# A four-layer conv/triangle kernel: one wait for PSUM banks moved, one sigmoid moved, and one layer's variance taken from whole float32 squares

## The chip, the cores and the metric

The kernel runs on one core of a Trainium2 chip. The metric is device time in microseconds (us), from the first to the last instruction and what lies around them. The median of three runs of the kernel before is 1442.51 us (1441.29 to 1446.19).

A core has five engines with instruction streams of their own, joined by semaphores: PE (TensorE, matrix products into PSUM), DVE (VectorE), ACT (ScalarE), POOL (GpSimd) and SP (the queue that starts DMAs). PSUM has eight banks.

## The reference

The image x has 192 x 192 positions of 64 channels in float32. Four layers are added to it in turn; each sees a group-normed copy. Cut to layer 1, whose kind the others share:

```
x = x + L1(_gn(x))                              # group norm, 32 groups of 2 channels
def L1(z):
    x = layernorm(z, ln_in_w, ln_in_b)          # over the 64 channels
    a = m * sigmoid(x @ w_a_g + b_a_g) * (x @ w_a_p + b_a_p)
    b = m * sigmoid(x @ w_b_g + b_b_g) * (x @ w_b_p + b_b_p)
    t = einsum('bikc,bjkc->bijc', a, b)
    t = layernorm(t, ln_out_w, ln_out_b) @ w_o + b_o
    return sigmoid(x @ w_g + b_g) * t
```

Layer 0 has the same form (its einsum in bf16), layer 2 has no mask and sums over the first index, layer 3 has no layer norm at its entry.

## The kernel before

Each layer l has three stages. **Phase A** normalises the input, makes the gate and the four projections and leaves `a` and `b` in SBUF (`lr`). **Phase b1** is the einsum, **phase b2** the second norm, the output product and the sum with x. The change touches phase A alone, and of it layers 0 to 2, which have the layer norm (`ln`).

Phase A runs over 48 tiles (`TILES`). A tile is two rows of the image (r = 0, 1), 2 x 192 positions in the free dimension; the 128 partitions are 64 channels of the upper and 64 of the lower half of the image. Each engine has a `step` that it runs for tile after tile, in an order written out by hand, which works ahead for later tiles. PE's steps are unrolled; the others loop over four tiles at a time, but for the first four and the last four. In step n:

- PE: the gate product of tile n (`gate`), the transposes that spread 1/deviation of tile n+1 over partitions (`spread`, L552), the projections of row 0 (`project(n, s, 0)`: a wide part L588, then a narrow part L598), the centring product of tile n+4 (`centre`, L520), the projections of row 1 (narrow, then wide), the variance of tile n+3 (L543).
- ACT: the gate's sigmoid (L804), `high` of tile n+1 (L821, the copy of the normalised tile that PE reads), the sigmoid of row 0 (L812), `centred` of tile n+4 (L784, writes `cen`), the sigmoid of row 1 (L812), the square of tile n+4 (L790).
- DVE: the masked product of row 1 of tile n-1 (`glu`, four instructions of L1065; L1072 in layer 2, one), variance plus epsilon of tile n+2 (L1031, `ve`), the normalising product of tile n+1 (L1041, `xn`), `sq_low` of tile n+3 (L1026), in layers 1 and 2 the low part of tile n+1 (L1048, `val`), the product of row 0 of tile n.
- POOL: the power -1/2 (L1224, `rstd`) and its spread over 64 columns (L1231, `rb`), tile n+2.

The variance on PE uses the squares (`sq`, stationary) against two columns of 1/64. So that bf16 products suffice, a square is taken as `sq_high`, the upper 16 bits of each word, and `sq_low`, the rest, which DVE computes. PE waits for it on `a_sq_lo`.

Row 0's projections lie in PSUM banks 4 and 5, row 1's in 6 and 7. `glu` of tile n frees them, and counts `a_free`: value l x 96 + m + 1 says that the row m - 2, the last user of row m's banks, is done. PE waits for it at two places: before row 0 for row 0's banks, and, in layers with a norm, before the last pass of row 0's wide part for those of row 1. Layers 1 and 2 have three passes (weights and data in high and low bf16 parts), layer 0 has one pass in float32, so that in layer 0 the first and the last pass are the same and both waits stand ahead of row 0. PE's gate product of tile n also waits for `cen` of tile n+3 (`a_cen`), since both write banks 0 and 1.

Of the kernel before, what the change touches and what calls it, by code (L numbers as in the profile page):

```python
# [25 lines left out]
P = 128  # L26
# [5 lines left out]
TILES = HALF // ROWS  # L32
# [8 lines left out]
SUBS = ROWS * TILES  # L41
GROUP = 4
GROUPS = C // GROUP
CHUNKS = TILE // P
LAYERS = 4
# [10 lines left out]
HAS_MASK = (True, True, False, True)  # L56
GATE_FIRST = (True, False, True, False)
LATE = 14
T_SCALE = (1.0, 1.0, 1.0 / N, 1.0)
Z_BANK = (0, 1, 6, 7)  # L60


def build_triangle_layers(nc, x_in, params, consts, mask3_k, mask3_row, x_out):
# [6 lines left out]
    with ExitStack() as ctx:  # L70
# [16 lines left out]
        sq = sb("sq", [P, 2, TILE])  # L87
# [52 lines left out]
        k_sel = k[:, K_SEL:K_SEL + 2]  # L140
# [331 lines left out]
        def _(pe):  # L472
# [19 lines left out]
            def phase_a(l):  # L492
# [44 lines left out]
                def variance(n, s):  # L537

                    slot_free(pe, a_ve, base + n)
                    pe.wait_ge(a_sq_lo, base + n + 1)  # L540
                    for j in range(CHUNKS):
                        for part in (sq_high, sq_low):
                            mm = nc.tensor.matmul(ps[:, 3, 2 * j:2 * j + 2],  # L543
                                                  part[:, s % 2, P * j:P * j + P], sel_bf[:, :],
                                                  start=part is sq_high, stop=part is sq_low)
                    mm.then_inc(a_var, 1)
# [27 lines left out]
                def project(n, s, r):  # L574
                    m = ROWS * n + r

                    if r == 0 or not ln:
                        pe.wait_ge(a_free, l * SUBS + m + 1)
                    banks = [ps[:, 4 + 2 * r + h, 0:2 * COLS].rearrange("p (v c) -> p v c", v=2) for h in range(2)]

                    def wide():
                        for w, x in passes:
                            start, stop = (w, x) == passes[0], (w, x) == passes[-1]
                            if ln and r == 0 and stop:

                                pe.wait_ge(a_free, l * SUBS + m + 2)
                            for h in range(2):
                                mm = nc.tensor.matmul(banks[h][:, :, 0:P], moving(x, s)[half(h), N * r:N * r + P],  # L588
                                                      proj_weights(w, h)[:, 0:2 * P], start=start, stop=stop,
                                                      skip_group_check=True)  # L590
                        return mm

                    def narrow():
                        for w, x in passes:
                            start, stop = (w, x) == passes[0], (w, x) == passes[-1]
                            for h in range(2):
                                for e in range(2):
                                    mm = nc.tensor.matmul(banks[h][TAIL * e:TAIL * e + TAIL, :, P:COLS],  # L598
                                                          moving(x, s)[half(h), N * r + P:N * r + N],
                                                          proj_weights(w, h)[:, 2 * P + P * e:3 * P + P * e],  # L600
                                                          start=start, stop=stop, skip_group_check=True)
                        return mm

                    if r == 0 or not ln:
                        wide()
                        mm = narrow()
                    else:
                        narrow()
                        mm = wide()
                    mm.then_inc(a_proj, 1)  # L610
# [161 lines left out]
        def _(act):  # L772
            def phase_a(l):
                base = l * TILES
                ln = HAS_LN[l]
                act.wait_ge(gn_dve, 7 * (l + 1))
                act.wait_ge(params_ready, l + 1)

                def centred(n, s):


                    act.wait_ge(a_z, base + n + 1)
                    slot_free(act, a_xn, base + n - RING + 1)
                    nc.scalar.activation(cen[:, s, :].rearrange("p (h j) -> p h j", h=2), ps[:, 0:2, 0:N], ACT.Identity,  # L784
                                         bias=gn_cb).then_inc(a_cen, 1)

                def squared(n, s):
                    act.wait_ge(a_cen, base + n + 1)
                    slot_free(act, a_var, base + n - 1)
                    nc.scalar.activation(sq[:, s % 2, :], cen[:, s, :], ACT.Square).then_inc(a_sq, 1)  # L790

                def plain(n, i, s):

                    act.wait_ge(in_loaded[s], in_count(l, s) + 16 * (i + 1))
                    slot_free(act, a_proj, l * SUBS + ROWS * (n - 1))
                    nc.scalar.activation(xn[:, s % 2, :], in_ring[:, s, :], ACT.Identity, bias=gn_b, scale=gn_a)\
                        .then_inc(a_xn, 1)

                def gate(n, i, s):
                    act.wait_ge(a_gate_mm, base + n + 1)  # L800

                    slot_free(act, gate_stored[s], 16 * (l * TURNS + i))
                    slot = gate_ring[:, s, :].rearrange("p (r j) -> p r j", r=ROWS)
                    nc.scalar.activation(slot if ln else gate_ring[:, s, :], ps[:, 0:2, N:2 * N] if ln else ps[:, 3, 0:TILE],  # L804
                                         ACT.Sigmoid, bias=gate_bias[:, 0:1]).then_inc(a_gate, 1)

                def sigmoids(n, s, r):
                    m = ROWS * n + r
                    act.wait_ge(a_proj, l * SUBS + m + 1)

                    act.wait_ge(a_free, l * SUBS + m + 1)
                    nc.scalar.activation(act_out[:, r, :].rearrange("p (h c) -> p h c", h=2),  # L812
                                         ps[:, 4 + 2 * r:6 + 2 * r, COLS:2 * COLS], ACT.Sigmoid).then_inc(a_sig, 1)

                def high(n, s):


                    act.wait_ge(a_xn, base + n + 1)
                    slot_free(act, a_proj, l * SUBS + ROWS * (n - 1))
                    out = xn_parts[:, s % 2, 0, :] if IN_PARTS[l] else val[:, s % 2, :]  # L820
                    nc.scalar.activation(out, xn[:, s % 2, :], ACT.Copy, bias=1.0).then_inc(a_hi, 1)  # L821

                def step(n, i, s, ahead):
                    gate(n, i, s)
                    if ln and ahead >= 1:
                        high(n + 1, (s + 1) % RING)
                    sigmoids(n, s, 0)
                    if ln and ahead >= 4:
                        centred(n + 4, s)
                    sigmoids(n, s, 1)  # L830
                    if ln and ahead >= 4:
                        squared(n + 4, s)
                    if not ln and ahead >= 2:
                        plain(n + 2, i + (s + 2) // RING, (s + 2) % RING)

                if ln:
                    for n in range(RING):
                        centred(n, n)
                        squared(n, n)
                    high(0, 0)  # L840
                else:
                    plain(0, 0, 0)
                    plain(1, 0, 1)
                over_tiles(act, step)
# [90 lines left out]
        def _(dve):  # L935
# [79 lines left out]
            def phase_a(l):  # L1015
                base = l * TILES
                ln = HAS_LN[l]
                out5 = lr_view(l).rearrange("p a e (h r) -> p h a e r", h=2)
                mask4 = mask[:, :, :].rearrange("p t (h r) -> p t h r", h=2)
                if l:  # L1020
# [56 lines left out]
                def step(n, i, s, ahead):  # L1077
                    if not (isinstance(n, int) and n == 0):
                        glu(n - 1, 1)
                    if ln and ahead >= 2:  # L1080
                        var_eps(n + 2, (s + 2) % RING)
                    if ln and ahead >= 1:
                        normalise(n + 1, (s + 1) % RING)
                    if ln and ahead >= 3:
                        square_low(n + 3, (s + 3) % RING)
                    if IN_PARTS[l] and ahead >= 1:
                        low(n + 1, (s + 1) % RING)
                    glu(n, 0)

                if ln:  # L1090
                    square_low(0, 0)
                    square_low(1, 1)
                    var_eps(0, 0)
                    var_eps(1, 1)
                    normalise(0, 0)
                    square_low(2, 2)
                if IN_PARTS[l]:
                    low(0, 0)
# [283 lines left out]
```

## Time and profile before

| | |
|---|---|
| median of the runs | 1442.51 us |
| time of the profiled execution, its span | 1443.26 us, 1441.0 us |
| PE, PEld, DVE, ACT, POOL busy | 82%, 47%, 68%, 63%, 36% |
| phase A of layer 0, of layer 1, of layer 2 | some 50 to 252 us, 393 to 581 us, 780 to 961 us |
| granted TensorE clock, mean | 0.962 |

"PEld" is the loading of weights into PE, which overlaps its products. A group's idle time is that of its engine just before it, with what ended it. Times of single instructions come from the timeline, whose stamps count from the start of the span. In the timeline instructions of one line that follow each other are merged into one row (x4, x8).

### The profile page before, as it was taken

To read this page: it belongs to the slowest core of one execution; us is meant where nothing else is said; L and a number is where in the kernel's file an instruction comes from. 1 tells how busy PE (TensorE), PEld (TensorE's weight loads), DVE (VectorE), ACT (ScalarE), POOL (GpSimd) and SP (SyncE) were. 2 spreads that over 40 slices of the span, in tenths; PEclk is the share of its full clock that TensorE was granted. 3 is DMA by queue.
4 is the path that set the end of the run, shared out by engine and by line. 5 is a ranking of instruction groups with operands and counts; after the bars stand their busy time and mean duration, and the time that the engine had idled before them with its cause. 6 is when DMAs were issued, how large, how long until landed. Compare 5 with 4: busy or idle time off the path is not lost. (4 is left out here: it accounts for less than half of the span.)

```text
span 1441.0 us, 43510 instructions
## 1 busy us (share of the span) xinstructions
PE 1182.2 (82%) x13502; PEld 679.1 (47%) x13502; DVE 978.2 (68%) x2692; ACT 905.7 (63%) x1849; POOL 524.0 (36%) x490
## 2 busy tenths in 40 slices
PE   0688887889778887999982888889888788899887
PEld 0355554444344444674431555557544344467443
DVE  6577777368789999226991877752299799931577
ACT  0566676389677776126992877752399677732676
POOL 0355554035465565003551666630055300000355
PEclk9999999899889999999995989999999899999999
DMA  8011111678633332697658555549889544459898
GB/s 293 23 51 51 45 51 51 153 213 265 208 97 110 111 103 82 200 298 216 200 162 323 159 160 155 168 138 297 274 279 286 189 154 153 153 175 314 272 303 272
DMA packets 222489, 259.67 MB, mean 180 GB/s; under 512 B 54176, under 2 KB 209056, under 8 KB 222368
## 3 DMA queue, kind: packets, MB, share of 16 engines
q1 hardware_dynamic: 193920, 232.75, 51.5%
q10 hardware_dynamic: 28448, 25.17, 5.3%
q8 instruction: 92, 1.51, 0.4%
q14 instruction: 29, 0.24, 0.1%
HBM read 139.89 MB, written 117.96 MB: 179 GB/s over the span
## 5 line engine op out<-in xcount | busy, mean ns | idle before, releaser
L1065 DVE SCALAR_TENSOR_TENSOR lr<-ps,mask,act_out 128x128 f32 (+5 forms) x1152 | 281.8, 310 | 66.8 <-ACT act_out L812 59.5
L1224 POOL TENSOR_TENSOR rstd<-ve,half_col 128x6 f32<-128x6 f32 x144 | 190.4, 1322 | 248.8 <-DVE ve L1031 247.4
L588 PE MATMUL ps<-w_parts,val 64*128 64x256 bf16 (+1 forms) x1728 | 202.5, 312 | 47.5 <-DVE lr L1065 47.4
L1269 POOL TENSOR_TENSOR new_ring<-val,lr 128x384 f32<-128x384 f32 x96 | 103.8, 1083 | 375.9 <-issue 301.4
L812 ACT ACTIVATE act_out<-ps 128x384 f32<-128x384 f32 x384 | 186.2, 487 | 52.0 <-PE ps L598 35.4
L1257 POOL TENSOR_TENSOR val<-act_out,gate_ring 128x384 f32<-128x384 f32 x96 | 100.1, 1043 | 221.7 <-ACT act_out L883 190.2
L821 ACT ACTIVATE val<-xn 128x384 bf16<-128x384 f32 (+1 forms) x144 | 75.3, 523 | 123.4 <-PE ps L598 63.0
L703 PE MATMUL ps<-in_ring,k 128*128 128x384 f32 x288 | 123.6, 514 | 26.2 <-DMA in_ring<-t_scratch 21.8
L866 ACT ACTIVATE sq<-ps 128x384 f32<-128x384 f32 x192 | 104.6, 545 | 53.1 <-PE ps L703 51.2
L1116 DVE COPY cen<-ps 128x384 f32<-128x384 f32 x48 | 26.7, 557 | 161.8 <-PE ps L661 161.8
L661 PE MATMUL ps<-lr 64*128 64x192 f32 (+3 forms) x896 | 128.3, 334 | 10.0 <-DVE lr L1065 5.2
L588 PEld LDWEIGHTS ps<-w_parts,val 64*128 64x128 bf16 (+1 forms) x1728 | 81.1, 115 | 111.1 <-DVE lr L1065 70.7
L1231 POOL TENSOR_TENSOR rb<-rstd,one_col 128x384 f32<-128x384 f32 x144 | 127.2, 884 | 11.3
L598 PE MATMUL ps<-w_parts,val 64*64 64x128 bf16 (+1 forms) x3456 | 130.4, 238 | 0.0
L1129 DVE TENSOR_TENSOR xn<-ps,rb 128x384 f32<-128x384 f32 x192 | 106.0, 552 | 32.3 <-ACT rb L877 31.8
L872 ACT ACTIVATE rb<-ps,eps_col 128x384 f32<-128x384 f32 x192 | 120.0, 625 | 9.5 <-PE ps L715 5.8
L661 PEld LDWEIGHTS ps<-lr 64*128 64x128 f32 (+3 forms) x896 | 105.9, 181 | 29.8 <-issue 18.4
L784 ACT ACTIVATE cen<-ps,gn 128x384 f32<-128x384 f32 x144 | 82.9, 576 | 52.4 <-PE ps L520 52.2
L804 ACT ACTIVATE gate_ring<-ps,gate_bias 128x384 f32<-128x384 f32 x192 | 111.2, 579 | 3.2 <-PE ps L520 2.7
L877 ACT ACTIVATE rb<-rb 128x384 f32<-128x384 f32 x192 | 109.4, 570 | 0.3
L598 PEld LDWEIGHTS ps<-w_parts,val 64*64 64x64 bf16 (+1 forms) x3456 | 84.2, 115 | 39.3 <-issue 25.0
L1158 DVE TENSOR_TENSOR sq_low<-sq 128x384 bf16<-128x384 f32 x144 | 79.7, 553 | 33.2 <-ACT sq L866 33.0
(110 smaller groups left out, 2195.0 us busy)
## 6 DMA issues: line engine op xcount, KB each, us to landing
gate_scratch<-gate_ring SPq DMA_DIRECT2D x192, 192.0 KB, 2.3
gate_ring<-gate_scratch SPq DMA_DIRECT2D x96, 384.0 KB, 3.9
lr<-x_scratch SPq DMA_DIRECT2D x72, 384.0 KB, 4.9
in_ring<-t_scratch SPq DMA_DIRECT2D x72, 384.0 KB, 3.8
x_scratch<-new_ring SPq DMA_DIRECT2D x48, 384.0 KB, 3.2
in_ring<-x_scratch SPq DMA_DIRECT2D x96, 192.0 KB, 2.4
lr<-x SPq DMA_DIRECT2D x6, 1536.0 KB, 15.5
t_scratch<-cen SPq DMA_DIRECT2D x96, 96.0 KB, 4.1
```

The costliest lines, as they stand in the source:

```text
L588: mm = nc.tensor.matmul(banks[h][:, :, 0:P], moving(x, s)[half(h), N * r:N * r + P], proj_weights(w, h)[:, 0:2 * P], start=start, stop=sto ...
L598: mm = nc.tensor.matmul(banks[h][TAIL * e:TAIL * e + TAIL, :, P:COLS], moving(x, s)[half(h), N * r + P:N * r + N], proj_weights(w, h)[:, 2 ...
L661: mm = nc.tensor.matmul(ps[:, b + i % 2, N * (i // 2):N * (i // 2) + N], left[:, 0:P], right, start=first and i < 2, stop=last and i >= 2, ...
L703: nc.tensor.matmul(ps[:, Z_BANK[s], 0:TILE], w_c, t_slots(l, s)[:, 0, :], start=True, stop=True).then_inc(b2_z, 1)
L804: nc.scalar.activation(slot if ln else gate_ring[:, s, :], ps[:, 0:2, N:2 * N] if ln else ps[:, 3, 0:TILE], ACT.Sigmoid, bias=gate_bias[:, ...
L812: nc.scalar.activation(act_out[:, r, :].rearrange("p (h c) -> p h c", h=2), ps[:, 4 + 2 * r:6 + 2 * r, COLS:2 * COLS], ACT.Sigmoid).then_i ...
L872: nc.scalar.activation(rb[:, s % 2, :], ps[:, 2 + s % 2, 0:TILE], ACT.Ln, bias=eps_col[:, l:l + 1]).then_inc(b2_log, 1)
L877: nc.scalar.activation(rb[:, s % 2, :], rb[:, s % 2, :], ACT.Exp, scale=-0.5).then_inc(b2_rstd, 1)
L1065: ins = nc.vector.scalar_tensor_tensor(out5[:, h, lo // 2:hi // 2, :, row], ps[:, 4 + 2 * r + g, lo:hi].rearrange("p (a e) -> p a e", e=2) ...
L1129: nc.vector.tensor_tensor(xn[:, s % 2, :], ps[:, Z_BANK[s], 0:TILE], rb[:, s % 2, :], ALU.mult)\
L1224: nc.gpsimd.tensor_tensor(rstd[:, s % 2, :], ve[:, s % 2, :], half_col[:, :], ALU.pow)\
L1231: nc.gpsimd.tensor_tensor(rb[:, s % 2, :].rearrange("p (a c) -> p a c", c=C), rstd[:, s % 2, :].rearrange("p (a o) -> p a o", o=1) .broadc ...
```

## The change

1. In `project`, the wait for row 1's banks moves from ahead of the last pass of row 0's wide part to ahead of row 1's projections.
2. In ACT's step, in layer 0 alone, the sigmoid of row 0 comes before `high` of the next tile.
3. In layer 1, PE takes the variance from the whole float32 squares: three float32 products per tile instead of six in bf16, waiting for ACT's square (`a_sq`). DVE makes no `sq_low` there.

```diff
+WHOLE_VAR = (False, True, False, False)
+LOWS = tuple(sum(1 for m in range(l) if not WHOLE_VAR[m]) for l in range(LAYERS))
...
                     slot_free(pe, a_ve, base + n)
-                    pe.wait_ge(a_sq_lo, base + n + 1)
+                    if WHOLE_VAR[l]:
+                        pe.wait_ge(a_sq, base + n + 1)
+                        for j in range(CHUNKS):
+                            mm = nc.tensor.matmul(ps[:, 3, 2 * j:2 * j + 2], sq[:, s % 2, P * j:P * j + P], k_sel,
+                                                  start=True, stop=True)
+                        mm.then_inc(a_var, 1)
+                        return
+                    pe.wait_ge(a_sq_lo, LOWS[l] * TILES + n + 1)
...
                     m = ROWS * n + r
-                    if r == 0 or not ln:
-                        pe.wait_ge(a_free, l * SUBS + m + 1)
+                    pe.wait_ge(a_free, l * SUBS + m + 1)
...
                             start, stop = (w, x) == passes[0], (w, x) == passes[-1]
-                            if ln and r == 0 and stop:
-
-                                pe.wait_ge(a_free, l * SUBS + m + 2)
...
                     gate(n, i, s)
+                    if l == 0:
+                        sigmoids(n, s, 0)
                     if ln and ahead >= 1:
                         high(n + 1, (s + 1) % RING)
-                    sigmoids(n, s, 0)
+                    if l:
+                        sigmoids(n, s, 0)
...
+                halved = ln and not WHOLE_VAR[l]
...
-                    if ln and ahead >= 3:
+                    if halved and ahead >= 3:
                         square_low(n + 3, (s + 3) % RING)
...
-                if ln:
+                if halved:
                     square_low(0, 0)
                     square_low(1, 1)
+                if ln:
                     var_eps(0, 0)
                     var_eps(1, 1)
                     normalise(0, 0)
+                if halved:
                     square_low(2, 2)
```

The next two lists are PE's stream in one step of layer 0, before and changed: the gate product of a tile (`val,w_gate`), the spread (`k,rb`), row 0, the centring (`lr,w_centre`), row 1. Line numbers of the changed kernel are higher by up to nine.

```order
L520 MATMUL ps<-val,w_gate 64x192 [waits a_cen,a_hi]
L520 MATMUL ps<-val,w_gate 64x192 x3
L552 MATMUL ps<-k,rb 128x128 [waits a_xn,a_rb]
L552 MATMUL ps<-k,rb 128x128 x2
L588 MATMUL ps<-w_parts,val 128x2x128 [waits a_free]
L588 MATMUL ps<-w_parts,val 128x2x128
L598 MATMUL ps<-w_parts,val 64x2x64 x4
L520 MATMUL ps<-lr,w_centre 64x192 [waits a_gate,a_cen]
L520 MATMUL ps<-lr,w_centre 64x192 x3
L598 MATMUL ps<-w_parts,val 64x2x64 x4
L588 MATMUL ps<-w_parts,val 128x2x128 x2
```

```order
L522 MATMUL ps<-val,w_gate 64x192 [waits a_cen,a_hi]
L522 MATMUL ps<-val,w_gate 64x192 x3
L561 MATMUL ps<-k,rb 128x128 [waits a_xn,a_rb]
L561 MATMUL ps<-k,rb 128x128 x2
L593 MATMUL ps<-w_parts,val 128x2x128 [waits a_free]
L593 MATMUL ps<-w_parts,val 128x2x128
L603 MATMUL ps<-w_parts,val 64x2x64 x4
L522 MATMUL ps<-lr,w_centre 64x192 [waits a_gate,a_cen]
L522 MATMUL ps<-lr,w_centre 64x192 x3
L603 MATMUL ps<-w_parts,val 64x2x64 [waits a_free]
L603 MATMUL ps<-w_parts,val 64x2x64 x3
L593 MATMUL ps<-w_parts,val 128x2x128 x2
```

The order of the products stays. The first `a_free` wait is still there but asks for one row less, and a second one stands behind the centring, ahead of row 1.

ACT's stream in one step of layer 0's loop, before and changed:

```order
L804 ACTIVATE gate_ring<-ps,gate_bias 128x384 [waits gate_stored1,a_gate_mm]
L266 REGISTER_ALU [waits a_xn]
L821 ACTIVATE val<-xn 128x384 [waits a_proj]
L809 REGISTER_ALU
L812 ACTIVATE act_out<-ps 128x384 [waits a_free,a_proj]
L782 REGISTER_ALU
L784 ACTIVATE cen<-ps,gn 128x384 [waits a_xn,a_z]
```

```order
L809 ACTIVATE gate_ring<-ps,gate_bias 128x384 [waits gate_stored1,a_gate_mm]
L814 ISA
L817 ACTIVATE act_out<-ps 128x384 [waits a_free,a_proj]
L826 ACTIVATE val<-xn 128x384 [waits a_proj,a_xn]
L787 REGISTER_ALU
L789 ACTIVATE cen<-ps,gn 128x384 [waits a_xn,a_z]
```

The sigmoid of row 0 (`act_out`) now stands ahead of `high` (`val<-xn`), and `cen` directly behind `high`.

PE's stream at the end of a step of layer 1, from the last projections over the variance to the next gate, before and changed:

```order
L588 MATMUL ps<-w_parts,val 128x2x128 x6
L543 MATMUL ps<-sel_bf,sq 128x2 [waits a_sq_lo,a_ve]
L543 MATMUL ps<-sel_bf,sq_low 128x2
L543 MATMUL ps<-sel_bf,sq 128x2
L543 MATMUL ps<-sel_bf,sq_low 128x2
L543 MATMUL ps<-sel_bf,sq 128x2
L543 MATMUL ps<-sel_bf,sq_low 128x2
L520 MATMUL ps<-val,w_gate_parts 64x192 [waits a_cen,a_lo]
```

```order
L593 MATMUL ps<-w_parts,val 128x2x128 x6
L545 MATMUL ps<-k,sq 128x2 [waits a_sq,a_ve]
L545 MATMUL ps<-k,sq 128x2 x2
L522 MATMUL ps<-val,w_gate_parts 64x192 [waits a_cen,a_lo]
```

Nothing moves here: the variance stays where it was, with three float32 products in the place of six.

## Rows read from the trace of the kernel before

**Rows 1.** Page, costliest groups: busy us, mean ns | idle before, releaser.
```profile
L588 PE MATMUL ps<-w_parts,val 64*128 64x256 bf16 (+1 forms) x1728 | 202.5, 312 | 47.5 <-DVE lr L1065 47.4
```

**Rows 2.** Windows, layer 0: us; busy PE, PEld, DVE, ACT, POOL; clock; DMA share; GB/s.
```profile
60.00:230.00 170.00, 142.35 (x2013) 86.26 (x2013) 124.17 (x455) 117.49 (x248) 88.71 (x83) 1.00 0.14 49
```

**Rows 3.** Timeline, layer 0, product of row 0: tiles 0, 43 and 47.
```profile
57.56 0.99 DVE L1065 SCALAR_TENSOR_TENSOR lr<-ps,mask,act_out 128x128 bf16<-128x128 f32 x4 [1.14 <-ACT act_out L812]
...
235.33 2.01 DVE L1065 SCALAR_TENSOR_TENSOR lr<-ps,mask,act_out 128x128 f32 x8 [0.96 <-ACT act_out L812]
...
250.29 1.89 DVE L1065 SCALAR_TENSOR_TENSOR lr<-ps,mask,act_out 128x128 bf16<-128x128 f32 x8 [1.82 <-ACT act_out L812]
```

**Rows 4.** Timeline, one step of layer 0: start us, us, instruction [idle before <-releaser].
```profile
145.11 0.21 PEld L520 LDWEIGHTS ps<-val,w_gate 64*64 64x64 f32 x8
...
145.59 0.31 PEld L552 LDWEIGHTS ps<-k,rb 128*128 128x128 f32 x3 [0.28 <-issue]
...
145.66 0.99 DVE L1065 SCALAR_TENSOR_TENSOR lr<-ps,mask,act_out 128x128 f32 x4 [0.17 <-ACT act_out L812]
...
146.57 0.15 DVE L1031 TENSOR_SCALAR ve<-ps 128x6 f32<-128x6 f32 x1
...
146.77 0.33 PEld L588 LDWEIGHTS ps<-w_parts,val 64*128 64x128 f32 x4 [0.86 <-DVE lr L1065]
...
147.30 0.52 ACT L821 ACTIVATE val<-xn 128x384 f32<-128x384 f32 x1 [0.94 <-DVE xn L1041]
147.43 0.21 PEld L598 LDWEIGHTS ps<-w_parts,val 64*64 64x64 f32 x8 [0.33 <-issue]
...
147.95 0.49 ACT L812 ACTIVATE act_out<-ps 128x384 f32<-128x384 f32 x1
...
148.21 0.83 POOL L1231 TENSOR_TENSOR rb<-rstd,one_col 128x384 f32<-128x384 f32 x1
148.34 0.57 ACT L784 ACTIVATE cen<-ps,gn 128x384 f32<-128x384 f32 x1
...
149.10 0.49 ACT L812 ACTIVATE act_out<-ps 128x384 f32<-128x384 f32 x1 [0.19 <-PE ps L588]
...
149.22 0.21 PEld L520 LDWEIGHTS ps<-val,w_gate 64*64 64x64 f32 x8
```

**Rows 5.** Timeline, one step of layer 1.
```profile
502.68 0.26 PEld L520 LDWEIGHTS ps<-val,w_gate_parts 64*64 64x64 bf16 x12 [0.45 <-DVE val L1048]
...
503.08 0.31 PEld L552 LDWEIGHTS ps<-k,rb 128*128 128x128 f32 x3
...
503.56 0.11 PEld L588 LDWEIGHTS ps<-w_parts,val 64*128 64x128 bf16 x4 [0.17 <-issue]
...
504.21 0.10 PEld L588 LDWEIGHTS ps<-w_parts,val 64*128 64x128 bf16 x2 [0.54 <-DVE lr L1065]
...
504.61 0.55 DVE L1026 TENSOR_TENSOR sq_low<-sq 128x384 bf16<-128x384 f32 x1
...
504.82 0.52 ACT L821 ACTIVATE val<-xn 128x384 bf16<-128x384 f32 x1 [0.99 <-PE ps L598]
...
505.25 0.47 ACT L812 ACTIVATE act_out<-ps 128x384 f32<-128x384 f32 x1
...
505.37 0.56 DVE L1048 SCALAR_TENSOR_TENSOR val<-xn,val 128x384 bf16<-128x384 f32 x1 [0.22 <-ACT val L821]
505.62 0.57 ACT L784 ACTIVATE cen<-ps,gn 128x384 f32<-128x384 f32 x1
505.65 0.10 PEld L543 LDWEIGHTS ps<-sel_bf,sq 128*128 128x128 bf16 x1 [0.21 <-issue]
...
506.31 0.26 PEld L520 LDWEIGHTS ps<-val,w_gate_parts 64*64 64x64 bf16 x12 [0.44 <-DVE val L1048]
```

**Rows 6.** Source line L480 (ns min/median/max); timeline of its two weight loads.
```profile
L480 PEld LDWEIGHTS ps<-cols,w_out x8: 191/192/333, 10.1 to 993.0; 128*128 128x128 f32 x8
...
615.77 0.30 PEld L480 LDWEIGHTS ps<-cols,w_out 128*128 128x128 f32 x2
```

## Prediction

> **What bounds the kernel now.** I read the costliest groups of the page first, to see where TensorE stands idle, and then the timeline of one step in layer 0 and in layer 1. The projections of line L588 are preceded by 47.5 us of idle PE time, 47.4 of it waits for the masked product L1065, which only layers 0 and 1 have [rows 1]; layer 2 (L1072) has the other 0.1, so nothing is to be had there. In layer 0 PE runs at a granted clock of 1.00 and is busy 142 of 170 us [rows 2], yet every tile costs the same 4.1 us, so some chain is closed.
>
> The timeline of layer 0 names it [rows 4]. I call G the gate matmuls (PEld L520 at 145.11), S the spread (L552, 145.59), W0 and N0 the wide and narrow parts of row 0 (L588 at 146.77, L598 at 147.43), N1 and W1 those of row 1, sig0 and sig1 the two L812, glu0 and glu1 the two L1065. W0 stands idle 0.86 us and starts 0.12 after glu1 of the previous tile ends (145.66 + 0.99 = 146.65). From W0 the chain runs through all of the projection to sig1 (149.10, 2.33 after W0), and the next glu1 stands one period after 145.66, at 149.77: 0.12 + 2.33 + 0.67 + 0.99 = 4.11 us. That is the period G to G (145.11 to 149.22). A single wait, put on row 0 for banks that only row 1 uses, closes it. ACT's high (L821) adds nothing on that chain, but it stands ahead of sig0 and waits for DVE's xn.
>
> In layer 1 the chain is another one [rows 5]. DVE's low (L1048, 505.37) waits for ACT's high (504.82), and sq_low (504.61, 0.55 long, over at 505.16) lies wholly in that time: DVE is idle 0.22 us between the two. sig0 (505.25) follows high by 0.43. The period, 506.31 − 502.68 = 3.63 us, is closed by DVE and this one trip to ACT: xn, high, low, glu0, glu1, and back. PE waits twice in it, at the third pass of row 0 (504.21, 0.54 us of idle weight load) and at the gate (506.31, 0.44), which stands 0.12 after cen (505.62 + 0.57), so I take cen for its releaser and not low.
>
> **Layer 0, the moved wait and the moved sigmoid.** W0 now waits for glu0 of the previous tile only. That ended before glu1 began (145.66), so W0 follows S. Layer 0 has no row for W0 unhindered; layer 1 has S to W0 = 503.56 − 503.08 = 0.48. PE's own work per tile is then 4.11 less the wait: 146.77 − (145.59 + 0.48) = 0.70, so 3.41 us. What is late next? The gate of the next tile waits for cen (L784), and cen now stands behind sig0 and high:
> - G to S 0.48, S to W0 0.48, W0 to N0 0.66, N0 to sig0 0.52 (147.95 − 147.43) [rows 4];
> - sig0 to high: back-to-back activations start 0.39 apart (147.95 to 148.34); high to the next one 0.43 (504.82 to 505.25) [rows 4, 5];
> - cen itself 0.57, and its release of the gate 0.12: 506.31 − (505.62 + 0.57) [rows 5].
>
> Sum 0.48 + 0.48 + 0.66 + 0.52 + 0.39 + 0.43 + 0.57 + 0.12 = 3.65 us. Other loops are shorter. Row 1's new wait stands behind N0 (G + 1.62) and the centre's matmuls; glu1 stands at (sig0 + 0.39 + 0.43 + 0.46) + 0.67 = G + 4.09 and ends at G + 5.08, which is 1.43 after the next G: before N0 even begins (0.46 for cen to sig1 is my estimate, between 0.43 and cen's own 0.57). Behind that wait stand N1, W1, the variance and the next gate, and nobody pays. The long path over POOL: ve to the end of rb is 149.04 − 146.57 = 2.47; ve starts 0.91 after glu1, at G + 5.00, so rb is there at G + 7.56, and the spread that wants it stands at 2 × 3.65 + 0.48 = 7.78. It fits by 0.2 us, and would bind at about 3.55. DVE's work is 124.2 us in 170, or 3.0 per tile [rows 2]. high is ready 0.73 after ve starts (147.30 − 146.57), at G + 5.73 − 3.65 = 2.08, and now starts at G + 2.53, so xn is waited for no more. High before sig0 would have put sig0 behind DVE's xn, so the moved sigmoid is part of the gain.
>
> How many tiles: glu0 of tile 0 stands at 57.56, of tile 43 at 235.33, of tile 47 at 250.29 [rows 3]. 43 steps average 4.134; 43 × (4.134 − 3.65) = 20.8 us. The last four steps have no centre; they took 14.96 us. There POOL's path comes in sight, I put them at 13.5, 1.4 less. Layer 0: **−22.2 us**.
>
> **Layer 1, sq_low and the whole squares.** DVE loses 48 sq_low of 0.55 us, 26 us of work, and I give it **nothing**: it is covered by ACT's high, and without it the wait before low grows from 0.22 to about 0.7 us. PE trades six bf16 products of two columns for three float32 ones. Nearest row: the product L480, 128×128 against one column, two loads in 0.30 us where a single one takes 0.19, so a load every 0.11 us; at the lower clock, where a load takes 0.33, I take twice that, 0.22 [rows 6]. Six loads are 0.66, with 0.09 for the turn to the gate 0.75 us. The room: the third pass no longer waits, so the variance moves from 505.65 to about 505.25 (0.40 is my estimate, less than the 0.54 of that row). cen lets the gate go at 506.31: room 1.06, need 0.75. **0 us**, with 0.3 to spare. Without the moved wait the room would be 0.66 and the gate 0.1 late. Bounds: below nothing is excluded, since no DVE or ACT instruction of the chain gets shorter; above, see the rivals. Every 0.1 us past 1.06 costs 4.4 us over the 44 steps that have a gate waiting for cen.
>
> Before the loop of layer 1 two variances at the slow clock stand on PE ahead of the first spread: 2 × 6 × 0.22 = 2.6 us against 0.3, partly in waits for POOL and with two sq_low gone; I put +0.7. At its end row 0 of the last tile no longer waits for glu1: −0.7. Together 0 ± 1.5.
>
> A rule that speaks against the change: the Trainium skill, "FP8 and Floating Point Precision", TensorE Precision Notes, says that a true float32 product takes four passes through the array. By that rule a product would have four loads, not two, and the sum would be the second rival's. The row of L480 lists two loads for it, not four.
>
> **The sum.** The profiled execution took 1443.26 us (span 1441.0), the median of the runs is 1442.51. 1443.3 − 22.2 + 0 = 1421.1, and on the scale of the median 1420.3. I say 1420.5.
>
> **Rivals.**
> - Less in layer 0, 1429: each of three ACT instructions that now waits in a row pays some 0.07 more in the loop, where register work stands between them, and the period is 3.85. For: DVE's L1065 starts 0.67 − 0.49 = 0.18 after the sigmoid ends. Against: 0.39 holds in the same loop. 43 × 0.28 + 1.4 = 13.6. Chance 0.14.
> - Dearer float32 products, 1436: 12 loads × 0.11 + 0.09 = 1.41 us, 0.35 past the room, 44 × 0.35 = 15 back. Chance 0.04.
> - **Slower**, 1478: the same place, but each of 12 loads keeps PE for its whole 0.19: 2.37 us, 1.31 past the room, 57 us back against 22. It decides from 1.06 + 22.2/44 = 1.56 us per variance. Against it: L480's loads start 0.11 apart. Chance 0.03.
> - PE alone bounds layer 0, 1410: 43 × (4.134 − 3.41) + 1.4 = 32.5. Needs cen earlier by 0.24. Chance 0.05.
> - The wait gives nothing, since row 1 waits at once for the same glu1: 1442. That would need glu1 to end some 0.5 us later than I placed it. Chance 0.02.
>
> My forecast (period 3.55 to 3.75, 1416 to 1426) has 0.72. The range 1413 to 1432 takes in the first rival and half of the fast one. A measurement tells 0.3% (4.3 us) from no change; faster is the forecast and the rivals at 1429, 1436 and 1410, 0.95, less 0.02 for a mechanism that I did not see: 0.93; same 0.03, slower 0.04.
>
> **What would show it.** In the after profile: layer 0's G to G 3.65; W0 with no wait for L1065; PE idle about 0.24 before the gate, released by ACT cen; sig0 ahead of high. Layer 1: period 3.63 as before, DVE idle 0.7 before low, the variance in six loads over about 0.66. It would be wrong if the first projection still waits for L1065, if layer 0's period is over 3.8, or if in layer 1 PE has no wait left and the period is over 3.7.

## The result and the profile after

The changed kernel took 1422.47 us (median of 4 runs, 1419.38 to 1431.3), the kernel before 1441.9 us in the same job (4 runs, 1438.09 to 1446.19). The ratio is 0.9862, with a 95% interval of 0.9826 to 0.9898: 1.4% faster. The forecast was 1420.5 us in a range of 1413 to 1432. The profiled execution took 1419.38 us, of which the span is 1417.1, so it is 23.9 us shorter than the one before; the mean granted clock was 0.962 in both. One execution of e5 below, its profiled one (1456.07 us), was in a slower state than all others; e5's ratio leaves it out, and of its profile only rows at the full granted clock are read.

From the page of the kernel after come the span, the engines' busy time and the two groups that answer to [rows 1] (busy us, mean ns | idle before, releaser):

```profile
span 1417.1 us, 43403 instructions
PE 1197.3 (84%) x13502; PEld 704.8 (50%) x13502; DVE 954.9 (67%) x2644; ACT 898.2 (63%) x1849; POOL 522.8 (37%) x490
L1074 DVE SCALAR_TENSOR_TENSOR lr<-ps,mask,act_out 128x128 f32 (+5 forms) x1152 | 282.0, 311 | 42.5 <-ACT act_out L817 34.8
L593 PE MATMUL ps<-w_parts,val 64*128 64x256 bf16 (+1 forms) x1728 | 194.0, 313 | 0.6 <-DVE lr L1074 0.5
```

The projections now stand behind 0.6 us of idle PE time, where they stood behind 47.5. DVE has 48 instructions fewer (2644 against 2692), the halving subtractions of layer 1.

The windows view of layer 0 after, with the columns of [rows 2]:

```profile
60.00:220.00 160.00, 152.48 (x2168) 92.33 (x2164) 132.77 (x487) 118.83 (x262) 94.98 (x89) 1.00 0.16 56
```

PE is busy 95% of the time where it was 84% (142.35 of 170), at the same granted clock of 1.00. The timeline of the products of row 0, tiles 0, 43 and 47, answers to [rows 3]:

```profile
57.61 0.99 DVE L1074 SCALAR_TENSOR_TENSOR lr<-ps,mask,act_out 128x128 bf16<-128x128 f32 x4 [1.13 <-ACT act_out L817]
...
213.92 2.12 DVE L1074 SCALAR_TENSOR_TENSOR lr<-ps,mask,act_out 128x128 f32 x8 [0.37 <-ACT act_out L817]
...
226.60 1.89 DVE L1074 SCALAR_TENSOR_TENSOR lr<-ps,mask,act_out 128x128 bf16<-128x128 f32 x8 [0.83 <-ACT act_out L817]
```

43 steps average (213.92 − 57.61)/43 = 3.635 us, and the last four take 12.68. From tile 0 to tile 47 that is 168.99 us against 192.73, 23.7 us less. That the span is 23.9 us shorter, nearly the same, is partly luck: between phase A of layer 0 and that of layer 1 the execution after took 2.0 us longer than the one before, and between those of layers 1 and 2 it took 3.4 us less, in stages that the change doesn't touch. One step of layer 0, the timeline that answers to [rows 4]:

```profile
145.27 0.82 POOL L1242 TENSOR_TENSOR rb<-rstd,one_col 128x384 f32<-128x384 f32 x1
...
145.76 0.24 PEld L522 LDWEIGHTS ps<-val,w_gate 64*64 64x64 f32 x8 [0.23 <-issue]
145.79 0.56 PE L522 MATMUL ps<-val,w_gate 64*64 64x192 f32 x8 [0.17 <-ACT cen L789]
146.21 0.99 DVE L1074 SCALAR_TENSOR_TENSOR lr<-ps,mask,act_out 128x128 f32 x4 [0.28 <-ACT act_out L817]
146.28 0.31 PEld L561 LDWEIGHTS ps<-k,rb 128*128 128x128 f32 x3 [0.28 <-POOL rb L1242]
146.76 0.30 PEld L593 LDWEIGHTS ps<-w_parts,val 64*128 64x128 f32 x4 [0.17 <-issue]
...
147.39 0.21 PEld L603 LDWEIGHTS ps<-w_parts,val 64*64 64x64 f32 x8 [0.33 <-issue]
...
147.91 0.49 ACT L817 ACTIVATE act_out<-ps 128x384 f32<-128x384 f32 x1 [0.92 <-PE ps L603]
148.29 0.52 ACT L826 ACTIVATE val<-xn 128x384 f32<-128x384 f32 x1
...
148.71 0.57 ACT L789 ACTIVATE cen<-ps,gn 128x384 f32<-128x384 f32 x1
148.83 0.83 POOL L1242 TENSOR_TENSOR rb<-rstd,one_col 128x384 f32<-128x384 f32 x1
149.17 0.49 ACT L817 ACTIVATE act_out<-ps 128x384 f32<-128x384 f32 x1
149.39 0.24 PEld L522 LDWEIGHTS ps<-val,w_gate 64*64 64x64 f32 x8 [0.23 <-issue]
```

Read it down the chain. W0 (146.76) starts 0.48 after the spread and waits for nobody, though glu1 of the tile before (146.21) is only half done. sig0 (147.91) stands ahead of high (148.29), and cen (148.71, over at 149.28) is followed 0.11 later by the next gate, which the PE row names as released by cen. The period is 149.39 − 145.76 = 3.63 us.

One step of layer 1, the timeline that answers to [rows 5], and the source view of the float32 variance (ns min/median/max) in place of [rows 6]:

```profile
474.83 0.26 PEld L522 LDWEIGHTS ps<-val,w_gate_parts 64*64 64x64 bf16 x12 [0.63 <-DVE val L1057]
...
475.71 0.22 PEld L593 LDWEIGHTS ps<-w_parts,val 64*128 64x128 bf16 x6 [0.17 <-issue]
...
476.98 0.52 ACT L826 ACTIVATE val<-xn 128x384 bf16<-128x384 f32 x1 [1.00 <-DVE xn L1050]
477.36 0.74 PEld L545 LDWEIGHTS ps<-k,sq 128*128 128x128 f32 x6 [0.21 <-issue]
...
477.53 0.56 DVE L1057 SCALAR_TENSOR_TENSOR val<-xn,val 128x384 bf16<-128x384 f32 x1 [0.69 <-ACT val L826]
477.78 0.57 ACT L789 ACTIVATE cen<-ps,gn 128x384 f32<-128x384 f32 x1
...
478.46 0.26 PEld L522 LDWEIGHTS ps<-val,w_gate_parts 64*64 64x64 bf16 x12 [0.36 <-DVE val L1057]
478.49 0.44 PE L522 MATMUL ps<-val,w_gate_parts 64*64 64x192 bf16 x12 [0.30 <-ACT cen L789]
```
```profile
L545 PEld LDWEIGHTS ps<-k,sq x288: 186/192/338, 373.6 to 547.9; 128*128 128x128 f32 x144
```

All three passes of W0 go at once, one group of six loads. DVE is idle 0.69 us before low where it was idle 0.22: the time of sq_low has become a wait for ACT. The variance takes 0.74 us and the gate still waits 0.36 after it. The row of its weight load names low, over at 478.09; cen is over at 478.35, 0.11 before the gate, and the row of its products names cen. The period is unchanged, 478.46 − 474.83 = 3.63 us. Every fourth step is longer (gate sigmoid to gate sigmoid 3.63, 3.63, 3.68, 3.91, before and after alike): that is the edge of the loop, whose body holds four tiles.

### The profile page after: what moved, and what is told of

It is laid out like the page before. It is cut to its first block and busy times, and to the rows that moved or that the text cites. A ratio compares the mean times of both kernels' runs of the same rounds, so it can differ in the third digit from the quotient of the medians.

```text
span 1417.1 us, 43403 instructions
## 1 busy us (share of the span) xinstructions
PE 1197.3 (84%) x13502; PEld 704.8 (50%) x13502; DVE 954.9 (67%) x2644; ACT 898.2 (63%) x1849; POOL 522.8 (37%) x490
## 5 line engine op out<-in xcount | busy, mean ns | idle before, releaser
L593 PE MATMUL ps<-w_parts,val 64*128 64x256 bf16 (+1 forms) x1728 | 194.0, 313 | 0.6 <-DVE lr L1074 0.5
L593 PEld LDWEIGHTS ps<-w_parts,val 64*128 64x128 bf16 (+1 forms) x1728 | 79.9, 115 | 47.5 <-issue 33.3
```

## The experiments

A step below is always from one gate sigmoid to the next at the full granted clock. Medians of different jobs are compared by their ratios to the kernel before in the same job, never directly.

**The change taken apart: e1 to e4.** e1 is the kernel before with the moved wait alone.

```diff
-                    if r == 0 or not ln:
-                        pe.wait_ge(a_free, l * SUBS + m + 1)
+                    pe.wait_ge(a_free, l * SUBS + m + 1)
...
-                            if ln and r == 0 and stop:
-                                pe.wait_ge(a_free, l * SUBS + m + 2)
```

> The moved wait alone, with the kernel before's order on ACT and its variance. Theory (two loops compete in layer 0): W0 stands behind S, but high stays ahead of sig0 and waits for DVE's xn, so the period becomes xn to high 0.66, high to sig0 0.43, sig0 to glu0 0.66, glu0 to glu1 0.95, glu1 to xn 0.98 = 3.68 us, and DVE's loop edge shows again (0.3 per four tiles): about 3.75, 43 x 0.38 = 16 us and the tail. I expect -15 to -19 us, some 1424. Rival (the wait alone is the whole gain, ACT's order is nothing): period 3.63, -20 to -22 us, and ACT cen releases the gate. Second rival (the wait and the sigmoid are both needed): period over 4.0, less than -5 us.

Measured: 1425.06 us against 1444.12, ratio 0.9873 (0.9857 to 0.9888). Its timeline, the gate of one step in layer 0:

```profile
143.43 0.57 ACT L780 ACTIVATE cen<-ps,gn 128x384 f32<-128x384 f32 x1
...
144.12 0.24 PEld L520 LDWEIGHTS ps<-val,w_gate 64*64 64x64 f32 x8 [0.22 <-issue]
144.15 0.56 PE L520 MATMUL ps<-val,w_gate 64*64 64x192 f32 x8 [0.16 <-ACT cen L780]
...
146.70 0.52 ACT L817 ACTIVATE val<-xn 128x384 f32<-128x384 f32 x1 [1.28 <-DVE xn L1037]
```

The wait alone already reaches the period of 3.62, closed by cen. From the first gate sigmoid of layer 0 to the last it took 174.63 us, the kernel before 192.97 and the changed one 170.46. The 4.2 us between e1 and the changed kernel lie in one step of four, the loop's edge: it takes 3.98 to 4.04 us in e1, 3.55 in the changed kernel. The last row shows what it is: at the edge high waits 1.28 us for DVE's xn, and sig0 and cen stand behind high; in the other steps high waits 0.90 us and PE's row 0 releases it. So the expectation had the size (some 1424) and a part of the mechanism: xn is the wait in one step of four, cen in the other three.

e2 is the kernel before with the moved sigmoid alone.

```diff
+                    if l == 0:
+                        sigmoids(n, s, 0)
                     if ln and ahead >= 1:
                         high(n + 1, (s + 1) % RING)
-                    sigmoids(n, s, 0)
+                    if l:
+                        sigmoids(n, s, 0)
```

> Only the order on ACT in layer 0: sig0 ahead of high, the wait where it was. Theory: the loop of 4.11 us (glu1, W0, all of the projection, sig1, glu1) stays, and sig1 is now behind sig0, high and cen: W0 + 0.66 + 0.52 + 0.39 + 0.43 + 0.46 = W0 + 2.46 instead of 2.33, so the period is 4.24 and the kernel 0.13 x 43 = 5 us slower, 1447. Rival (sig0 earlier always helps): period under 4.11, faster.

Measured: 1449.1 us, ratio 1.0035 (1.0019 to 1.0051). By itself this part of the change costs 5 us, as expected. The waits view of its layer 0 (60 to 220 us; us in total, times, longest) and two rows of its timeline:

```profile
PEld ps L588 <- DVE lr L1068: 28.0, 38, 0.8
```
```profile
143.80 0.24 PEld L520 LDWEIGHTS ps<-val,w_gate 64*64 64x64 f32 x8 [0.23 <-issue]
...
148.02 0.24 PEld L520 LDWEIGHTS ps<-val,w_gate 64*64 64x64 f32 x8 [0.23 <-issue]
```

The period is 4.22: the loop over glu1 is still closed. Its sig1 follows W0 by 2.44 us (145.35 to 147.79) where it was 2.33, for in the new order high and cen start after sig0 and sig1 after them.

e3 is the whole float32 squares alone, e4 the wait and the sigmoid without them (all four entries of `WHOLE_VAR` False).

> Only layer 1's variance from whole float32 squares, without sq_low; wait and order as before. Theory (sq_low is covered by ACT's high; the float32 loads lie in PE's wait for cen): layer 1's period stays 3.63, DVE's idle before low grows from 0.22 to 0.7, the gate comes up to 0.15 late and nobody pays: 1442 +- 2. Rival (DVE's work counts): 44 x 0.48 = -21 us. Second rival (the float32 loads eat more than the room of 0.66): period up by 0.1 or more, +4 us or more.

> The change without its part in layer 1: moved wait and moved sigmoid, six bf16 products and sq_low in layer 1. Theory: all of the gain is layer 0's, so it is like the changed kernel: layer 0's period 3.63, layer 1's 3.63, -20 to -22 us, 1420 to 1423. Rival (the whole squares carry part of the gain): less than -17 us, with layer 1 longer than in the changed kernel by 4 us or more.

Measured: e3 1446.74 us, ratio 1.0017 (1.0003 to 1.0032); e4 1424.42 us, ratio 0.9853 (0.9834 to 0.9873). Between e4 and the changed kernel (0.9862, 0.9826 to 0.9898) the intervals show no difference: the whole gain is layer 0's. The squares give nothing, and by themselves they cost a little: e3's interval lies above 1, by 0.4 to 4.6 us.

The profiles show where. In e3 the steps of layer 1's loop are as before (four take 14.84 us, before 14.85), so what the float32 variance took beyond its six bf16 products cost no time there. The cost lies ahead of the loop and in its first steps. From the layer's first `cen` to its first gate sigmoid it takes 10.7 us in each of the seven profiles with whole squares here and below (e5 not counted), and 9.8 us in each of the six without. The first four steps took 14.54, 16.98 and 17.30 us in three profiles with whole squares (the changed kernel, after_again below, e3), and 14.40 to 15.05 in the four without them and with the same orders in layer 1 (before, e1, e2, e4). In these steps the granted clock differed, which the windows views of the same part of the loop show, first the kernel before, then e3:

```profile
404.00:418.00 14.00, 12.54 (x262) 7.69 (x260) 13.01 (x44) 10.51 (x25) 7.47 (x8) 0.93 0.33 100
```
```profile
406.00:420.00 14.00, 14.00 (x201) 9.47 (x198) 8.69 (x30) 9.06 (x20) 6.01 (x6) 0.67 0.23 69
```

The changed kernel had 4.42 and 3.26 us in the first two steps in one execution, and 5.75 and 4.59 in another (run again as after_again); over the 10 us from the first gate on the mean granted clock was 0.89 in the one and 0.58 in the other. So the clock rises at different moments with the same program. That part of the cost can't be given a size from a single profile; the 0.9 us ahead of the first gate can.

**How much room the float32 variance has: e5.** The three products are issued twice.

```diff
-                        for j in range(CHUNKS):
+                        for j in list(range(CHUNKS)) * 2:
```

> The changed kernel with the three float32 variance products of layer 1 made twice (the second set writes the same numbers). Theory (PE has a room of 1.06 us in layer 1's period, and beyond it every 0.1 us costs 4.4): the step's work up to the variance is 2.53 in the changed kernel's trace, 12 loads at 0.11 and the turn make 1.4 to 1.5, so the period is 3.95 to 4.05, 0.3 to 0.4 over 3.63: +10 to +16 us on the changed kernel, 1431 to 1438. Rival (PE has ample room): no change. Rival (each load keeps PE for 0.19): period over 4.7, +45 us.

Measured: 1433.5 us against 1439.61, ratio 0.9961 (0.9943 to 0.9979), which is 0.0099, or some 14 us, above the changed kernel's 0.9862, as expected (10 to 16). Two rows at the full granted clock:

```profile
522.41 1.42 PEld L545 LDWEIGHTS ps<-k,sq 128*128 128x128 f32 x12 [0.21 <-issue]
523.84 0.23 PEld L522 LDWEIGHTS ps<-val,w_gate_parts 64*64 64x64 bf16 x12
```

The gate follows at once and waits for nobody: twelve loads are past the room, by 0.3 us (3.93 against 3.63 in a plain step). Four steps take 15.73 us, four times 3.93, against 14.85: where PE closes the loop, its edge costs nothing, and the mean step is 0.22 us longer. In the changed kernel cen lets the gate go 478.46 − 477.36 = 1.10 us after the variance starts, and its six loads need 0.74.

**Is DVE's idle time before low worth anything: e6 to e8.** In e6 layer 1 too has the sigmoid ahead of high, and DVE does low behind the product of row 0 instead of ahead of it.

```diff
-                    if l == 0:
+                    if l <= 1:
                         sigmoids(n, s, 0)
...
-                    if l:
+                    if l > 1:
                         sigmoids(n, s, 0)
...
+                    if l == 1 and ahead >= 1:
+                        glu(n, 0)
+                        low(n + 1, (s + 1) % RING)
+                        return
```

> The changed kernel, and in layer 1 also sig0 ahead of high on ACT, and on DVE low of the next tile behind glu0 instead of ahead of it. Theory (DVE's trip to ACT and back closes layer 1's loop): glu0 now covers ACT's high, DVE's idle 0.69 before low goes, the period falls from 3.63 to what PE needs, 2.53 + 0.75 + 0.1 = about 3.35 (DVE's own work is 3.0): 44 x 0.28 = 12 us and part of the loop edges, 1406 to 1411. Rival (another wait takes its place: the gate then waits for low, which stands 1 us later): period 3.6, no change. Rival: slower than the changed kernel, since low ends only at glu0 + 0.95 + 0.56 and PE's gate waits on it.

Measured: 1430.14 us, ratio 0.9937 (0.9913 to 0.9961). I had expected 12 us less and got a layer 1 that is 11 us longer (184.19 from first to last gate sigmoid, the changed kernel 173.02). The last rival held, that low ends too late and the gate waits for it. Its timeline:

```profile
474.12 0.99 DVE L1074 SCALAR_TENSOR_TENSOR lr<-ps,mask,act_out 128x128 f32 x4 [0.76 <-ACT act_out L817]
...
475.03 0.55 DVE L1057 SCALAR_TENSOR_TENSOR val<-xn,val 128x384 bf16<-128x384 f32 x1
...
475.63 0.23 PEld L522 LDWEIGHTS ps<-val,w_gate_parts 64*64 64x64 bf16 x12 [0.62 <-DVE val L1057]
```

The gate now waits for low. The loop is glu0 to low 0.91, low to gate 0.60, gate to spread 0.37, to W0 0.48, to N0 0.43, to sig0 0.42, to glu0 0.66: 3.87 us. The wait before low is gone, and a longer loop has been bought for it: 3.87 us in a plain step where it was 3.63, and 15.48 in four steps where it was 14.85. e7 is e6 with `WHOLE_VAR` False again, e8 is e6 with the same orders in layer 2.

> The previous kernel with the bf16 variance and sq_low back in layer 1. Theory (the whole squares give nothing while high covers sq_low, but they do where it is laid open): DVE's work per tile is 3.0 + 0.48 = 3.5 and the loop edge shows, so the period is 3.5 to 3.55 against 3.35: 6 to 9 us slower than the previous kernel. Rival (sq_low stays hidden): equal within 2 us. Second rival (PE bounds, and six bf16 products are 0.5 shorter): faster than the previous kernel.

> As the kernel with low late in layer 1, and the same two orders in layer 2, whose variance stays in bf16. Theory: layer 2 waits in part for its gathered input (DMA), its steps that don't are 3.24 us with PE waiting 0.4 for cen; 0 to -6 us on the kernel with low late in layer 1. Rival: layer 2 is bounded by its DMA throughout, no change within 1 us.

Measured: e7 1423.04 us (0.9893, 0.9856 to 0.993) with the same period of 3.87, e8 1430.42 us (0.9943, 0.9915 to 0.997). e8's layer 2 took 166.35 us from first to last gate sigmoid, e6's 164.33 and e7's 166.21, so the orders gave nothing there. e7 was expected slower than e6 and its layer 1 is not (182.19): with the loop over PE closed at 3.87, sq_low is hidden once more. Its median is 7 us below e6's, though their intervals meet. Some 2.8 us of that are the price of the whole squares at the layer's start: e7 has 0.9 us less ahead of the first gate and 1.9 less in the first four steps (16.16 against 18.01). The rest stays open.

**Filling the time of high: e10 to e12.** If DVE's loop xn, high, low, glu0, glu1 closes layer 1, half of glu1 can be done while ACT makes high. e10 cuts the product of row 1 in two, one half ahead of ve and xn, one behind, and has PE do the variance ahead of row 1's projection. after_again is the changed kernel in the same job.

```diff
+                    if l == 1 and ahead >= 3:
+                        variance(n + 3, (s + 3) % RING)
                     project(n, s, 1)
-                    if ln and ahead >= 3:
+                    if ln and l != 1 and ahead >= 3:
                         variance(n + 3, (s + 3) % RING)
...
-                        glu(n - 1, 1)
+                        glu(n - 1, 1, (0,) if l == 1 else (0, 1))
...
                         normalise(n + 1, (s + 1) % RING)
+                    if tail and l == 1:
+                        glu(n - 1, 1, (1,))
```

> The changed kernel once more, as the measure for the two beside it: 1419 to 1425, 20 to 22 us below the kernel before; periods of 3.63 in layers 0 and 1.

> The changed kernel with two orders changed in layer 1: on DVE the masked product of row 1 is split, two instructions ahead of ve and xn and two behind xn, where they cover ACT's high; on PE the variance stands ahead of row 1's projections. Theory: the loop xn, high, low, glu0, glu1 loses the 0.48 us of the two moved instructions; what is then late is PE's own work, 2.53 + 0.83 = 3.36, and the loop from W1 over sig1, half of glu1 and xn back to the wait of N1 is 3.24. Period 3.36 to 3.45, 44 x 0.2 = 8 to 12 us faster than the changed kernel, about 1412. Rival (N1 now waits for the late half of glu1, as the gate did for low in the other order): period 3.63 or more, no gain or up to 6 us slower.

> The previous kernel with six bf16 products and sq_low in layer 1. Theory (once high's time is filled, sq_low is no longer covered, and the whole squares pay): DVE's work is 3.0 + 0.48 = 3.5 us a tile and its loop edge adds 0.3 every four, so the period is 3.5 to 3.6: 4 to 9 us slower than the previous kernel. Rival (PE's load was the bound, bf16 is 0.5 shorter): faster than the previous kernel.

Measured: after_again 1419.1 us (0.9844, 0.9793 to 0.9895), e10 1412.11 us (0.9821, 0.9773 to 0.987), e11, which is e10 with the halved squares, 1424.37 us (0.9897, 0.9866 to 0.9929). One step of e10 in layer 1, DVE's rows, then ACT's and the weight loads:

```profile
475.98 0.54 DVE L1077 SCALAR_TENSOR_TENSOR lr<-ps,mask,act_out 128x128 f32 x2 [0.21 <-ACT act_out L819]
...
476.51 0.56 DVE L1052 TENSOR_TENSOR xn<-ps,cen 128x384 f32<-128x384 f32 x1
476.99 0.54 DVE L1077 SCALAR_TENSOR_TENSOR lr<-ps,mask,act_out 128x128 f32 x2
477.76 0.56 DVE L1059 SCALAR_TENSOR_TENSOR val<-xn,val 128x384 bf16<-128x384 f32 x1 [0.23 <-ACT val L828]
```
```profile
471.60 0.23 PEld L522 LDWEIGHTS ps<-val,w_gate_parts 64*64 64x64 bf16 x12 [0.21 <-issue]
...
471.71 0.49 ACT L819 ACTIVATE act_out<-ps 128x384 f32<-128x384 f32 x1 [0.34 <-PE ps L593]
...
472.10 0.52 ACT L797 ACTIVATE sq<-cen 128x384 f32<-128x384 f32 x1
...
472.51 0.57 ACT L811 ACTIVATE gate_ring<-ps,gate_bias 128x384 f32<-128x384 f32 x1
472.88 0.20 PEld L603 LDWEIGHTS ps<-w_parts,val 64*64 64x64 bf16 x12 [0.21 <-issue]
...
473.19 0.24 PEld L522 LDWEIGHTS ps<-in_ring,w_centre 64*64 64x64 f32 x8
...
473.71 0.74 PEld L545 LDWEIGHTS ps<-k,sq 128*128 128x128 f32 x6 [0.28 <-issue]
...
474.47 0.20 PEld L603 LDWEIGHTS ps<-w_parts,val 64*64 64x64 bf16 x12
...
474.76 0.22 PEld L593 LDWEIGHTS ps<-w_parts,val 64*128 64x128 bf16 x6
...
475.19 0.24 PEld L522 LDWEIGHTS ps<-val,w_gate_parts 64*64 64x64 bf16 x12 [0.21 <-issue]
...
475.31 0.49 ACT L819 ACTIVATE act_out<-ps 128x384 f32<-128x384 f32 x1 [0.24 <-PE ps L593]
```

DVE's idle time before low is 0.23 us, not 0.69. The gate waits for nobody, the steps are 3.60 us each and the long fourth one is gone, so four steps take 14.40 us instead of 14.85. The forecast was a period of 3.36 to 3.45, bounded by PE. It is not PE alone that bounds it now, but a loop of PE and ACT. The centring product waits for the gate's sigmoid (`a_gate`), since both products write banks 0 and 1; ACT makes that sigmoid behind sig1 and the square. The rows give the loop: sig1 to square 0.39, to gate sigmoid 0.41, its 0.57 and 0.11 to the centring product, to variance 0.52, to N1 0.76, to W1 0.29, to the next sig1 0.55: 3.60 us. In the steps of e10 from 440 to 480 us the centring product stands 0.11 or 0.12 after the end of that sigmoid each time, and 0.29 to 0.32 after N0. In the changed kernel it stands 0.26 to 0.31 after the sigmoid and 0.14 after N0, so that it waits for nobody there. With 0.17 us less for this wait PE's own work in e10 is 3.42 us, near the expected 3.36; the new place of the variance costs it some 0.06. What the sigmoid ahead of the square would give was not run.

Whether e10 as a whole beats the changed kernel the medians don't settle, for the intervals overlap; what is shown is 0.11 us per step of layer 1, some 5 us over 44 steps, of which the slow first steps (6.07, 5.90, 4.36) take back most in this execution (172.67 us for the layer, the changed kernel 173.02). The mean granted clock in the 10 us from its first gate on was 0.50.

Between e10 and e11 the whole squares have a worth at last: the steps of e11 are 3.86, 3.87, 3.86 and 3.98, layer 1 took 180.68 us, 8.0 more. The expected period was 3.5 to 3.6, from DVE's own work, and that was not the reason. With the variance ahead of row 1, PE waits there for sq_low, and row 1 waits behind it:

```profile
475.75 0.16 PE L552 MATMUL ps<-sel_bf,sq 128*128 128x2 bf16 x1 [0.86 <-DVE sq_low L1037]
```

The loop is sig1 to glu1 0.67, to xn 0.53, to the second half of glu1 0.47, to sq_low 0.45, to variance 0.67, to N1 0.24, to W1 0.30, to sig1 0.54: 3.87 us. So the worth of the whole squares here is that sq_low drops out of this loop, which the variance's place had closed.

e12 has PE's part of e10 alone.

> The changed kernel with only PE's part of the split: in layer 1 the variance stands ahead of row 1's projections; DVE's order as in the changed kernel. Theory (the split product opened DVE's loop, and the variance's new place costs PE about 0.3 us a tile, since the narrow products of row 0, the centring and those of row 1 no longer overlap): PE's work is 3.60, still under DVE's loop, so layer 1's steps are 3.63, 3.63, 3.68, 3.91 as in the changed kernel, within 2 us of it. Rival (the variance's place alone gave the 3.60 without a loop edge): layer 1 shorter by 4 us. Rival (PE and DVE now stop each other): steps of 3.7 or more.

Measured: 1420.82 us against 1439.56, ratio 0.9872 (0.9839 to 0.9905). Four steps take 14.92 us (3.63, 3.71, 3.81, 3.77), the changed kernel's 14.85: the sum is the expected one, the single steps are not. The order on PE by itself gives nothing, so the split product is needed for e10's 3.60. Whether it would do as well with the variance in its old place was not run. In e12 the gate's sigmoid is over 0.17 to 0.30 us before the centring product, and N0 to centring is 0.14 in most steps, although the variance stands in e10's place. So that place is not what made the 0.31 of e10.

## Why the prediction was right, point by point

- **Layer 0's period.** Forecast 3.65, measured 3.635 over 43 steps. The terms: G to S 0.52 (0.48), S to W0 0.48 (0.48), W0 to N0 0.63 (0.66), N0 to sig0 0.52 (0.52), sig0 to high 0.38 (0.39), high to cen 0.42 (0.43), cen 0.57 (0.57), release 0.11 (0.12). The next wait was the one named, cen's.
- **POOL's path.** "It fits by 0.2 us" held, and was tight: rb is over at 146.09 (145.27 + 0.82), the spread starts at 146.28, and the profile names rb as its releaser. It costs nothing yet: G to S is 0.52 only because the gate's loads start 0.03 ahead of its products here, and from the products it is 0.49 (145.79 to 146.28), as before (145.11 to 145.60). The forecast's own terms for rb add up to G + 7.47 (5.00 + 2.47), not 7.56; the rows show 7.59.
- **The tail.** Forecast 13.5 for the last four steps, measured 12.68. Without the centre's matmuls the products stand 3.49, 3.20, 3.27 and 2.72 us apart. With the loop that made layer 0 23.7 us shorter against 22.2.
- **The moved sigmoid.** "High before sig0 would have put sig0 behind DVE's xn, so the moved sigmoid is part of the gain": this step was right for one step in four and wrong for the rest. e1 has the old order and the same 3.62 in a plain step, since xn was early enough; at the loop's edge its high does wait for xn. What the move gives is that edge, some 4 us in the profiled layer 0, and by itself it costs 5 (e2). In the runs e1 and e4 can't be told apart (0.9873 and 0.9853).
- **sq_low, nothing.** Held: DVE idle 0.69 before low (0.7), the period 3.63, and e4 without this part is as fast.
- **The float32 variance.** Six loads in 0.74 (0.66 forecast, and 0.09 for the turn), room 1.10 (1.06), start at G + 2.53 (2.57). The rivals with twelve loads fell by the row of L545, two loads a product; e5 shows that with twelve loads the period would have been 3.93, by the sum of the prediction 3.63 + 1.41 − 1.06 = 3.98. The rule of the Trainium skill, "FP8 and Floating Point Precision", TensorE Precision Notes, on four passes for a true float32 product does not show here as four weight loads: the view lists 288 of them for 144 products.
- **Layer 1's ends.** Put at +0.7 and −0.7, together 0 ± 1.5. Both held: the start, first `cen` to first gate sigmoid, grew from 9.82 to 10.71 us, and the end, last gate sigmoid to the end of the last product, fell from 4.36 to 3.67. Missing was a term for the steps behind the first gate: the first four took 0.1 us more in the profiled execution and 2.6 more in after_again.
- **The sum.** Forecast −22.2 in a profiled execution; the spans differ by 23.9, the medians by 19.4. Layer 0 alone gave 23.7 against 22.2, of which 0.7 is the period and 0.8 the tail. The interval of the ratio, times 1441.9, is 14.7 to 25.1 us and holds both.

## What to carry to other kernels

A wait written for two users of a buffer belongs in front of the one whose data it guards: one wait for banks of the second row, put before the first, closed a loop over three engines and cost 18 us of 1441, though no engine was full. Work taken from an engine that waits at once for another (sq_low) buys nothing while no closed loop runs through it; before moving an instruction to fill it, add up the loop that its consumer closes, as e6's 3.87 shows. A row marked with no wait can still hide one, when the engine's next rows overlap: e10's centring product was found only by setting its start beside the end of what it waits for. Where parts of a change touch the same loop, time each alone: here one gave some 18 us, one cost 5 us alone and gave up to 4 behind the other, and the third gave nothing and cost a little at the layer's start.

## What the runs showed that was not expected

- A float32 load of 128×128 takes 0.19 us, and in a row they start about 0.11 apart (six in 0.74, twelve in 1.42); six bf16 loads of W0 all pass in 0.22. The float32 variance costs PE about 0.5 us more per tile than the bf16 one, hidden only where the gate waits anyway.
- With DVE's loop opened (e10), the next one was not PE's own work but the loop from row 1 over sig1, the square and the gate's sigmoid to the centring product, 3.60 us. It was in no forecast.
- The loop's edge cost 0.28 us in every fourth step of the changed kernel's layer 1 (3.91 against 3.63), whose loop runs over DVE and ACT, and 0.37 in e1's layer 0 (3.99 against 3.62). It cost nothing where PE closes the loop (e5: 15.73 in four steps of 3.93) and in e10 (3.60 in all four).
- The moment when the granted clock rises at layer 1's start varies between executions of one program: the first step of the changed kernel took 4.42 us in one and 5.75 in another.
